# A four-stage hybrid kernel: the opening of its attention stage put in another order

## The chip, the cores and the metric

The kernel runs on one core of a Trainium2 chip. The metric is the device time of one execution in microseconds (us); lower is better. The core has five engines that each work through their own instruction list in order: TensorE (PE, matrix products and transposes), VectorE (DVE), ScalarE (ACT), GpSimd (POOL), and SyncE (SP), which here only issues DMA transfers. They wait for one another by semaphores.

## The reference

The input x has 4 x 1024 tokens of 256 channels. Four stages follow, each with a layer norm ahead and added to x: attention, a gated recurrence, a delta-rule stage, the recurrence again. Only attention is touched:

```python
c_kv = x @ W_dkv.T
q = (x @ W_dq.T @ W_uq.T).reshape(B, T, 16, 16)
q_lat = einsum('bqhd,hdl->bhql', q, k_eff)      # k_eff = (W_dq.T @ W_uq.T @ W_uk) per head
attn = softmax(causal(einsum('bhql,bkl->bhqk', q_lat, c_kv) / 4))
y_lat = einsum('bhqk,bkl->bhql', attn, c_kv)
y = einsum('bhql,hld->bqhd', y_lat, v_eff)
```

## The kernel before

The tokens are 8 groups of 512 (`GROUPS`), two to a batch row b. The 16 heads are taken four at a time (`HPU`); a unit u = (b, four heads), 16 units in all. Channels 0 to 127 (mt = 0) hold the heads of units 0 and 1 of a batch row, channels 128 to 255 (mt = 1) those of units 2 and 3.

**A group's projection** (`project(g)`) is a list of items: two "turn" (transposes of the normed tokens into a_xT), two "lat" (a_lat: two 512-column products of two steps each, n = 0 and 1), four "qk" (queries, which = 0, and keys, which = 1, for either mt; queries need lat 0, keys need lat 1), and two "v". Ahead of it a "norm" item: DVE takes statistics (`bn_stats`, `bn_aggr`, four of each), POOL turns them into four normed tiles.

**A qk item** is number i in the order in which the items come. PE writes it to a PSUM bank; ACT copies its leading bf16 part (`hi`, a_parts slot 0); DVE subtracts that (`rest`, into a_rest[i % 2]); ACT copies the middle part (`mid`, slot 1); POOL makes the last (`lo`, slot 2); SP sends the three parts from a_parts[i % 4] to memory (`parts_out`, 384 KB). `hi(i)` waits for `parts_out(i - 4)`, and `rest(i)` for `lo(i - 2)`.

**A unit's stack** (q_stack, k_stack: six bf16 partial products laid out over 96 rows) is loaded back from memory by `load(u, halves)` on SP: 12 transfers of 64 KB for one half of the tokens, of 128 KB for both. It waits until the parts of its groups have landed. A "max" item multiplies the stacks for a block of scores and DVE reduces the maxima: 38 items a unit, the first 11 of which need only half 0. "negmax" then turns the negated maxima (PE), splits them in three parts (DVE) and SP writes them into q_stack (`max_in`). After it come the scores, the exponentials (ACT) and the values.

**The order** is written out in `order()`: all engines walk the list `prologue` first, then the lists in `during`, one for each score step. The prologue holds the projections of groups 0 and 1, then 46 max items (all of unit 0, eight of unit 1) with the projections of groups 2 and 3 laid between, and the first negmax. Each engine takes from an item what is its own and keeps the list's order, so an engine that waits for one item holds up all behind it, DMA issues on SP included. Banks are dealt to items in turn, seven in the prologue.

DVE begins with two casts (`constants_vector`, L176 and L177), then three memsets of ones rows in k_stack (L777) and one of a PSUM bank (L778), and only then takes the first item.

Of the kernel before, what the change touches and what calls it, by code (L numbers as in the profile page):

```python
# [11 lines left out]
ACT = mybir.ActivationFunctionType  # L12
AXIS_X = mybir.AxisListType.X

P = 128
# [3 lines left out]
KT = C // P  # L19
# [5 lines left out]
NH, HS = 16, 16  # L25
HPU = 4
# [3 lines left out]
STACKS = 3  # L30
# [223 lines left out]
class Attention:  # L254
# [4 lines left out]
    WEIGHTS = (("wdqT", [P, KT, P]), ("wdkvT", [P, KT, P]), ("wuqT", [P, C]), ("wuq", [P, KT, P]),  # L259
               ("wuk", [P, KT, P]), ("wdq", [P, C]), ("wuv", [P, KT, P]), ("woT", [P, KT, C]))  # L260
    ARRIVES = {n: ("in_tokens", "in_keys", "in_values")[i // 3] for i, (n, _) in enumerate(WEIGHTS)}
    PROJECTED = tuple((which, mt) for which in range(2) for mt in range(KT))
    SPLIT = ((0, 1, 0, 1, 2, 0), (0, 0, 1, 1, 0, 2))
    PRODUCTS, ROWS, MAX_ROWS = 6, 6 * HS, 3
    LEAD = 8
# [52 lines left out]
    def order(self):  # L318

        per = len(self.pairs)  # L320
        maxima = []
        for u in range(len(self.units)):
            maxima += [("max", u, w) for w in range(per)]
        late = {}
        for u in range(len(self.units)):
            late[min((u + 1) * per + 2, len(maxima)) - 1] = ("negmax", u)

        def project(g):
            return ([("turn", g, kt) for kt in range(KT)] + [("lat", g, n) for n in range(2)] +
                    [("qk", g, *p) for p in self.PROJECTED] + [("v", g, j) for j in range(0, TPG, 2)])  # L330

        def take(n):
            out = []
            for i in range(self.taken, min(n, len(maxima))):
                out += [maxima[i]] + ([late[i]] if i in late else [])
            self.taken = max(self.taken, min(n, len(maxima)))
            return out

        self.taken, lead = 0, per + self.LEAD
        more = project(2) + [("norm", 4)] + project(3)  # L340
        self.prologue = [("norm", 0), ("norm", 1), ("const", 0), ("const", 1), ("const", 2)] + project(0) + [("norm", 2)]
        self.prologue += project(1) + [("norm", 3)]
        for i in range(lead):
            self.prologue += take(i + 1) + more[i * len(more) // lead:(i + 1) * len(more) // lead]
        self.score_bank, self.score_free, at = {}, {}, 0
        for n, heads in enumerate(self.scored):
            for i in range(len(heads)):
                self.score_bank[n, i] = self.SCORE_BANKS[at % 3]
                at += 1
        self.during = [[] for _ in range(len(self.steps) + 4)]  # L350
        for g in range(4, GROUPS):
            first = 4 + (g - 4) * 22
            for i, item in enumerate(project(g)):
                self.during[first + 2 * i].append(item)
            if g > 4:
                for j in range(2):
                    self.during[first - 8 + 2 * j].append(("norm", g, slice(2 * j, 2 * j + 2)))
        for n, (u, kb, qc) in enumerate(self.steps):
            self.during[n] += take(lead + -(-per * (n + 1) // len(self.unit_steps)))
            if kb == (qc + 1) * TPG - 1:  # L360
                self.during[n + 3].append(("out", u, qc))
        s, self.bank, self.released, held, at = self.s, {}, {}, {}, 0
        for ring, items in [(self.PROLOGUE_BANKS, self.prologue)] + [(self.RING, items) for items in self.during]:
            for item in items:
                if item[0] != "norm":
                    b = ring[at % len(ring)]
                    at += 1
                    self.bank[item] = b
                    self.released[item] = held.get(b)
                    held[b] = self.release(item)  # L370
            if items is self.prologue:
                for n, heads in enumerate(self.scored):
                    for i in range(len(heads)):
                        self.score_free[n, i] = held.get(self.score_bank[n, i])
                        held[self.score_bank[n, i]] = s["exp"](n, i)
# [13 lines left out]
        return s[{"turn": "xT_out", "lat": "lat_out", "v": "v_out", "max": "max_red", "negmax": "max_rest", "out": "att_o"}[kind]](*a)  # L389

    def part(self, g, which, mt):
        return (g * 2 + which) * KT + mt

    def stack_free(self, u):

# [21 lines left out]
    def sync(self, e, unmet):  # L417
        k, s, io = self.k, self.s, self.k.io

        def load(u, halves):  # L420
            b, g = self.units[u]
            st = u % STACKS
            cols = slice(halves[0] * BANK, (halves[-1] + 1) * BANK)
            sent = [s[f"parts_out{i % 4}"](i) for h in halves for i in range(self.part(2 * b + h, 0, 0), self.part(2 * b + h + 1, 0, 0))]
            for n in range(len(self.SPLIT[0])):
                for which, dst in ((0, self.qst[st]), (1, self.kst[st])):
                    src = io["parts"][which, self.SPLIT[which][n], g * HPU * HS:(g + 1) * HPU * HS,
                                      b * T + cols.start:b * T + cols.stop].rearrange("(h d) t -> d h t", h=HPU)
                    for w in unmet(self.stack_free(u), s["k_ones"](st), *sent):
                        e.wait_ge(*w)  # L430
                    e.dma_start(dst[n * HS:(n + 1) * HS, :, cols], src).then_inc(*s[f"stack_in{st}"].did(u, halves[-1], n, which))
# [25 lines left out]
        k.load_x_sync(e, range(2, GROUPS))  # L457
        for item in self.prologue:
            send(item)
            if item == ("qk", 0, *self.PROJECTED[-1]):  # L460
                load(0, (0,))
            if item == ("qk", 1, *self.PROJECTED[-1]):
                load(0, (1,))
                for u in range(1, STACKS):
                    load(u, (0, 1))
        for n, items in enumerate(self.during):
# [172 lines left out]
    def scalar(self, e, unmet):  # L639
        k, s, bank, w_ = self.k, self.s, self.k.bank, self.w  # L640

        def copy_out(item):
            kind, a = item[0], item[1:]
            if kind not in ("const", "turn", "lat", "qk", "v"):
# [14 lines left out]
            if kind == "turn":  # L659
                g, kt = a  # L660
# [3 lines left out]
            if kind == "lat":  # L664
                g, n = a
# [4 lines left out]
            if kind == "qk":  # L670
                i = self.part(*a)
                for w in unmet(s["qk_mm"](i), s[f"parts_out{i % 4}"](i - 4) if i >= 4 else None):
                    e.wait_ge(*w)
                if a[0] >= self.EARLY:
                    for w in unmet(s["lo"](i - 2)):
                        e.wait_ge(*w)
                    e.activation(self.rest[i % 2][:, :], out[:, :], ACT.Copy).then_inc(*s["raw"].did(i))
                    return
                e.activation(self.parts[i % 4][:, 0, :], out[:, :], ACT.Copy).then_inc(*s["hi"].did(i))
                for w in unmet(s["rest"](i)):  # L680
                    e.wait_ge(*w)
                e.activation(self.parts[i % 4][:, 1, :], self.rest[i % 2][:, :], ACT.Copy).then_inc(*s["mid"].did(i))
            if kind == "v":
                g, j = a
                for w in unmet(s["v_mm"](g, j), s["v_ones"]()):
                    e.wait_ge(*w)
                e.activation(self.v_rows[:, g * TPG + j:g * TPG + j + 2, :, 0:HS],
                             out[:, :].rearrange("p (i h d) -> p i h d", i=2, h=NH), ACT.Copy).then_inc(*s["v_out"].did(g, j))

        def exps(n, i):  # L690
            width, heads = self.span(n)[1], self.scored[n][i]
            for w in unmet(s["scores"](n, i), s["values"](n - 2) if n >= 2 else s["veff_mm"]()):
                e.wait_ge(*w)
            e.activation(self.weights[n % 2][:, heads[0]:heads[-1] + 1, 0:width],  # L694
                         bank[self.score_bank[n, i]][:, 0:len(heads) * width].rearrange("p (h x) -> p h x", h=len(heads)),
                         ACT.Exp, scale=HS ** -0.5).then_inc(*s["exp"].did(n, i))
# [21 lines left out]
    def vector(self, e, unmet):  # L718
        k, s, bank = self.k, self.s, self.k.bank
# [53 lines left out]
                                rs[:, :, :].rearrange("p i (h o) -> p i h o", o=1).to_broadcast([P, TPG, HPU, HS]), ALU.mult  # L773
                                ).then_inc(*s["att_o"].did(u, qc))

        for st in range(STACKS):
            e.memset(self.kst[st][self.ROWS:self.ROWS + self.MAX_ROWS, :, :], 1.0).then_inc(*s["k_ones"].did(st))  # L777
        e.memset(bank[7][:, :], 0.0).then_inc(*s["o_zero"].did())  # L778
        for item in self.prologue:
            take(item)  # L780
        for items in self.during:
            for item in items:
                take(item)
# [829 lines left out]
def build(nc, io):  # L1613
    with ExitStack() as ctx:
        k = Kernel(nc, ctx, io)
        attention = Attention(k)
        first = Ffn(k, "f1_", attention.updated, attention.ends())
        delta = Delta(k, first.updated, first.ends())
        second = Ffn(k, "f2_", delta.updated, delta.ends())
# [19 lines left out]
                stage.scalar(e, unmet)  # L1639

        def vector(e, unmet):
            k.constants_vector(e, unmet)
            for stage in stages:
                stage.vector(e, unmet)

# [69 lines left out]
```

## Time and profile before

| | |
|---|---|
| time before, median of 3 runs | 1452.52 us (1448.99 to 1452.66) |
| time of the profiled execution | 1452.64 us |
| its span in the trace | 1450.8 us |
| PE busy | 1218.1 us, 84% of the span |
| DVE busy | 880.1 us, 61% |
| ACT busy | 610.2 us, 42% |
| POOL busy | 447.5 us, 31% |

The span is the stretch that the profiler's rows cover; 1.84 us of the execution lie around it. The busy times are averages over stages that are limited by different things, so the opening, some 112 us, has to be read for itself.

### The profile page before, as it was taken

To read this page: it belongs to the slowest core of one execution; us is meant where nothing else is said; L and a number is where in the kernel's file an instruction comes from. 1 tells how busy PE (TensorE), PEld (TensorE's weight loads), DVE (VectorE), ACT (ScalarE), POOL (GpSimd) and SP (SyncE) were. 2 spreads that over 40 slices of the span, in tenths; PEclk is the share of its full clock that TensorE was granted. 3 is DMA by queue.
4 is the path that set the end of the run, shared out by engine and by line. 5 is a ranking of instruction groups with operands and counts; after the bars stand their busy time and mean duration, and the time that the engine had idled before them with its cause. 6 is when DMAs were issued, how large, how long until landed. Compare 5 with 4: busy or idle time off the path is not lost. (4 is left out here: it accounts for less than half of the span.)

```text
span 1450.8 us, 32359 instructions
## 1 busy us (share of the span) xinstructions
PE 1218.1 (84%) x13530; PEld 755.3 (52%) x13530; DVE 880.1 (61%) x1900; ACT 610.2 (42%) x1207; POOL 447.5 (31%) x663
## 2 busy tenths in 40 slices
PE   3779999999999999989999346566987858699993
PEld 1434444444444444337888323245665647488882
DVE  4466767676788777715434755677867362354346
ACT  1426666666666766655222322122332212142222
POOL 2420505142200000014231556443663313342304
PEclk7889999999999999999999768778999979899996
DMA  5492535344455333000000000011111100000003
GB/s 153 131 148 90 89 45 89 56 78 67 73 63 62 49 45 45 2 1 1 1 0 1 17 17 10 21 32 29 33 29 32 35 25 12 2 1 0 1 1 116
DMA packets 78754, 61.66 MB, mean 43 GB/s; under 512 B 41360, under 2 KB 65552, under 8 KB 78480
## 3 DMA queue, kind: packets, MB, share of 16 engines
q1 hardware_dynamic: 77456, 57.18, 21.9%
q10 hardware_dynamic: 1152, 2.41, 0.5%
q8 instruction: 106, 1.74, 0.5%
q14 instruction: 40, 0.33, 0.1%
HBM read 38.20 MB, written 20.97 MB: 41 GB/s over the span
## 5 line engine op out<-in xcount | busy, mean ns | idle before, releaser
L694 ACT ACTIVATE weights<-psum 128x512 f32<-128x512 f32 (+1 forms) x608 | 322.4, 585 | 159.4 <-PE psum L607 157.5
L739 DVE TENSOR_REDUCE maxima<-psum 128x1 f32<-128x512 f32 (+3 forms) x432 | 262.2, 662 | 57.4 <-PE psum L538 56.3
L607 PE MATMUL psum<-q_stack,k_stack 99*128 99x512 bf16 (+3 forms) x768 | 223.7, 328 | 1.3 <-ACT weights L694 1.1
L538 PE MATMUL psum<-k_stack,q_stack 96*128 96x512 bf16 (+3 forms) x768 | 213.0, 328 | 5.8 <-DMA k_stack<-qk_parts 4.1
L624 PE MATMUL psum<-weights,v_rows 128*17 128x512 f32 (+3 forms) x1536 | 162.0, 494 | 0.1
L510 POOL TENSOR_TENSOR residual<-residual,att_o 128x256 f32<-128x256 f32 x32 | 23.2, 725 | 364.0 <-DVE att_o L772 364.0
L900 PE MATMUL psum<-f_xT,f_weights_hi 128*128 128x512 f32 x384 | 123.5, 403 | 0.0
L739 DVE TENSOR_REDUCE negmax<-psum 128x1 f32<-128x384 f32 (+3 forms) x176 | 102.3, 634 | 27.8 <-PE psum L538 26.2
L607 PEld LDWEIGHTS psum<-q_stack,k_stack 99*128 99x128 bf16 x768 | 72.5, 98 | 83.1 <-ACT weights L694 38.6
L965 ACT ACTIVATE f_gates<-psum,ffn_biases 128x512 f32<-128x512 f32 x72 | 49.7, 690 | 155.8 <-PE psum L906 155.8
L1335 PE MATMUL psum<-d_w_qkb,d_hT 128*128 128x260 f32 x128 | 48.0, 510 | 68.3 <-DVE d_attnT_k_kb_v L1505 57.8
L538 PEld LDWEIGHTS psum<-k_stack,q_stack 96*128 96x128 bf16 x768 | 72.4, 99 | 56.9 <-issue 7.9
L906 PE MATMUL psum<-f_state_parts,f_weights_hi 128*128 128x512 f32 x288 | 90.4, 395 | 0.0
L603 PE MATMUL psum<-identity,mask_scores 128*128 128x128 bf16 (+2 forms) x352 | 87.1, 248 | 3.7 <-DMA q_stack<-max_parts 2.7
L534 PE MATMUL psum<-mask_scores,identity 128*128 128x128 bf16 (+2 forms) x352 | 86.7, 246 | 2.3 <-DVE a_rest L730 1.2
L603 PEld LDWEIGHTS psum<-identity,mask_scores 128*128 128x128 bf16 x352 | 34.0, 97 | 96.1 <-ACT weights L694 58.3
L900 PEld LDWEIGHTS psum<-f_xT,f_weights_hi 128*128 128x128 f32 x384 | 71.8, 191 | 16.2
L900 PE MATMUL psum<-f_xT,f_weights_lo 128*128 128x512 f32 x192 | 76.4, 398 | 0.0
L1340 PE MATMUL psum<-d_w_vg,d_hT 128*128 128x512 f32 x128 | 75.7, 724 | 0.0
L1335 PEld LDWEIGHTS psum<-d_w_qkb,d_hT 128*128 128x128 f32 x128 | 27.6, 239 | 77.0 <-DVE d_attnT_k_kb_v L1505 42.7
L1056 DVE COPY f_hidden<-psum 128x512 f32<-128x512 f32 x16 | 11.0, 690 | 91.4 <-PE psum L918 91.4
L906 PEld LDWEIGHTS psum<-f_state_parts,f_weights_hi 128*128 128x128 f32 x288 | 54.1, 188 | 13.3
(165 smaller groups left out, 2277.9 us busy)
## 6 DMA issues: line engine op xcount, KB each, us to landing
qk_parts<-a_parts SPq DMA_DIRECT2D x32, 384.0 KB, 3.6
q_stack<-qk_parts SPq DMA_DIRECT2D x90, 128.0 KB, 7.1
k_stack<-qk_parts SPq DMA_DIRECT2D x90, 128.0 KB, 7.8
residual<-in_x SPq DMA_DIRECT2D x8, 512.0 KB, 7.5
out_x<-residual SPq DMA_DIRECT2D x8, 512.0 KB, 3.8
ffn_weights<-in_ffn_w ACTq DMA_DIRECT2D x1, 2048.0 KB, 9.1
systems<-d_a_rows SPq DMA_DIRECT2D x32, 64.0 KB, 1.8
d_systems<-systems SPq DMA_DIRECT2D x4, 512.0 KB, 4.8
```

The lines of the kernel that those rows point to most:

```text
L534: e.matmul(out[:, 0:len(heads) * width].rearrange("p (h x) -> p h x", h=len(heads))[:, :, width - P:width], k.ident16[:, :], k.mask16[:, : ...
L538: m = e.matmul(out[:, i * width:(i + 1) * width], self.qst[st][0:self.ROWS, h, qb * P:(qb + 1) * P], self.kst[st][0:self.ROWS, h, k0:k0 + ...
L603: e.matmul(out[:, 0:len(heads) * width].rearrange("p (h x) -> p h x", h=len(heads))[:, :, 0:P], k.mask16[:, :], k.ident16[:, :].rearrange( ...
L607: m = e.matmul(out[:, j * width:(j + 1) * width], self.kst[st][0:self.ROWS + self.MAX_ROWS, h, kb * P:(kb + 1) * P], self.qst[st][0:self.R ...
L624: m = e.matmul(bank[7][32 * h:32 * h + HS + 1, off:off + width], self.v_rows[:, b * QB + kb, g * HPU + h, :], self.weights[n % 2][:, h, 0: ...
L694: e.activation(self.weights[n % 2][:, heads[0]:heads[-1] + 1, 0:width], bank[self.score_bank[n, i]][:, 0:len(heads) * width].rearrange("p ...
L739: e.tensor_reduce(to, bank[self.bank[item]][:, 0:len(heads) * width].rearrange("p (h x) -> p h x", h=len(heads)), AXIS_X, ALU.max, negate= ...
L900: m = e.matmul(bank[bk][:, :], w_hi_lo[wp][:, gate, kt, ms], x[:, v, kt, :], start=q == 0, stop=t == 0 and q == len(self.TERMS) - 1)
L906: m = e.matmul(bank[bk][:, :], w_hi_lo[wp][:, 4 + gate, kt, ms], self.state_parts[j][:, v, kt, :], start=False, stop=q == len(self.TERMS) - 1)
L965: e.activation(gs[:, gate, mt, :], next_bank()[:, :], func, bias=(k.ffn_b if t else self.bias0)[:, gate, mt:mt + 1]).then_inc(*s["gate"].d ...
L1335: m = e.matmul(qk_bank[:, 0:NQ + DH], cols[kt], self.w_qkb[:, kt, :], start=kt == 0, stop=kt == KT - 1)
L1340: m = e.matmul(vg_bank[:, :], cols[kt], self.w_vg[:, kt, :], start=kt == 0, stop=kt == KT - 1)
```

## The change

1. DVE takes the statistics of groups 0 and 1 first; casts and memsets come after them.
2. The projections of groups 0 and 1 are laid into one another, and the statistics of group 2 come earlier among them.
3. The four qk items of a group come in the order (queries mt 0, keys mt 0, queries mt 1, keys mt 1) instead of (queries 0, queries 1, keys 0, keys 1), and `part` numbers them so.
4. ACT's middle part of an item is put off until ACT has done the next item's leading part (or the next lat or v copy).
5. A stack's load waits only for the parts with its own channel half, two to a group instead of four, and unit 0's two loads are issued right behind the second qk item of groups 0 and 1.

```diff
-    PROJECTED = tuple((which, mt) for which in range(2) for mt in range(KT))
+    PROJECTED = tuple((which, mt) for mt in range(KT) for which in range(2))
...
-        self.prologue = [("norm", 0), ("norm", 1), ("const", 0), ("const", 1), ("const", 2)] + project(0) + [("norm", 2)]
-        self.prologue += project(1) + [("norm", 3)]
+        first, second = project(0), project(1)
+        self.prologue = [("norm", 0), ("norm", 1), ("const", 0), ("const", 1), ("const", 2)] + first[:4] + second[:2]
+        self.prologue += first[4:6] + second[2:4] + [("norm", 2)] + first[6:] + second[4:] + [("norm", 3)]
...
     def part(self, g, which, mt):
-        return (g * 2 + which) * KT + mt
+        return (g * KT + mt) * 2 + which
...
-            sent = [s[f"parts_out{i % 4}"](i) for h in halves for i in range(self.part(2 * b + h, 0, 0), self.part(2 * b + h + 1, 0, 0))]
+            mt = g * HPU * HS // P
+            sent = [s[f"parts_out{i % 4}"](i) for h in halves for i in (self.part(2 * b + h, which, mt) for which in range(2))]
...
-            if item == ("qk", 0, *self.PROJECTED[-1]):
+            if item == ("qk", 0, 1, 0):
                 load(0, (0,))
+            if item == ("qk", 1, 1, 0):
+                load(0, (1,))
             if item == ("qk", 1, *self.PROJECTED[-1]):
-                load(0, (1,))
                 for u in range(1, STACKS):
                     load(u, (0, 1))
...
+        behind = []
+
+        def middle():
+
+            for item in behind:
+                i = self.part(*item[1:])
+                for w in unmet(s["rest"](i)):
+                    e.wait_ge(*w)
+                e.activation(self.parts[i % 4][:, 1, :], self.rest[i % 2][:, :], ACT.Copy).then_inc(*s["mid"].did(i))
+            behind.clear()
...
                 e.activation(self.parts[i % 4][:, 0, :], out[:, :], ACT.Copy).then_inc(*s["hi"].did(i))
-                for w in unmet(s["rest"](i)):
-                    e.wait_ge(*w)
-                e.activation(self.parts[i % 4][:, 1, :], self.rest[i % 2][:, :], ACT.Copy).then_inc(*s["mid"].did(i))
+                middle()
+                behind.append(item)
+                return
...
+            middle()
...
-        for st in range(STACKS):
-            e.memset(self.kst[st][self.ROWS:self.ROWS + self.MAX_ROWS, :, :], 1.0).then_inc(*s["k_ones"].did(st))
-        e.memset(bank[7][:, :], 0.0).then_inc(*s["o_zero"].did())
         for item in self.prologue:
             take(item)
+            if item == ("norm", 1):
+                k.constants_vector(e, unmet)
+                for st in range(STACKS):
+                    e.memset(self.kst[st][self.ROWS:self.ROWS + self.MAX_ROWS, :, :], 1.0).then_inc(*s["k_ones"].did(st))
+                e.memset(bank[7][:, :], 0.0).then_inc(*s["o_zero"].did())
...
         def vector(e, unmet):
-            k.constants_vector(e, unmet)
             for stage in stages:
                 stage.vector(e, unmet)
```

VectorE, the start of its list (a minus is a row of before, a plus one of the change):

```order
+L221 BN_STATS ln_stats<-residual 128x6 x4
+L225 BN_AGGR ln_moments<-ln_stats 128x2 x4
+L221 BN_STATS ln_stats<-residual 128x6 x4
+L225 BN_AGGR ln_moments<-ln_stats 128x2 x4
 L176 CAST identity<-identity 128x128
 L177 CAST mask_scores<-mask_scores 128x128
-L777 MEMSET k_stack 3x4096 x3
-L778 MEMSET psum 128x512
-L221 BN_STATS ln_stats<-residual 128x6 x4
-L225 BN_AGGR ln_moments<-ln_stats 128x2 x4
-L221 BN_STATS ln_stats<-residual 128x6 x4
-L225 BN_AGGR ln_moments<-ln_stats 128x2 x4
```

Both groups' statistics moved from behind the memsets to the very start.

ScalarE, the parts of group 0 in the kernel before (a_parts with a number is the buffer; from psum is a leading part, from a_rest a middle part):

```order
L679 ACTIVATE a_parts0<-psum0 128x512 [waits a_qk_mm]
L682 ACTIVATE a_parts0<-a_rest0 128x512 [waits a_rest]
L679 ACTIVATE a_parts1<-psum0 128x512 [waits a_qk_mm]
L682 ACTIVATE a_parts1<-a_rest1 128x512 [waits a_rest]
L679 ACTIVATE a_parts2<-psum1 128x512 [waits a_qk_mm]
```

And after the change, the first items of group 1 (qk items 4, 5 and 6):

```order
L693 ACTIVATE a_parts0<-psum1 128x512 [waits a_parts_out0,a_qk_mm]
L693 ACTIVATE a_parts1<-psum2 128x512 [waits a_parts_out1,a_qk_mm]
L653 ACTIVATE a_parts0<-a_rest0 128x512 [waits a_rest]
L693 ACTIVATE a_parts2<-psum2 128x512 [waits a_parts_out2,a_qk_mm]
L653 ACTIVATE a_parts1<-a_rest1 128x512 [waits a_rest]
```

The middle part of an item now stands behind the leading part of the next: that of item 5 behind a wait for the transfer of item 2.

SyncE, from the first transfer of parts on, after the change (L441 sends parts, L433 loads a stack; before, all four parts went ahead of the loads):

```order
L441 DMA qk_parts<-a_parts0 128x3x512 [waits a_lo,a_mid,a_hi]
L441 DMA qk_parts<-a_parts1 128x3x512 [waits a_lo,a_mid,a_hi]
L433 DMA q_stack0<-qk_parts 16x4x512 [waits a_parts_out1,a_parts_out0,a_k_ones]
...
L441 DMA qk_parts<-a_parts2 128x3x512 [waits a_lo,a_mid,a_hi]
L441 DMA qk_parts<-a_parts3 128x3x512 [waits a_lo,a_mid,a_hi]
```

The parts of items 2 and 3 moved behind the 12 issues of unit 0's first load. The same follows in group 1: items 4 and 5, 12 issues, items 6 and 7, then 24 issues for units 1 and 2.

## Rows read from the trace of the kernel before

**Rows 1.** Windows: each engine's busy time, granted TensorE clock (PEclk), DMA share, rate.

```profile
58.20:98.90 40.70, 32.64 (x130) 16.18 (x128) 28.18 (x58) 13.39 (x24) 15.26 (x21) 0.87 0.91 138
98.90:104.70 5.80, 0.39 (x5) 0.13 (x3) 2.74 (x5) 1.71 (x3) 1.15 (x1) 0.86 0.79 259
140.00:500.00 360.00, 359.95 (x2694) 162.13 (x2692) 267.94 (x519) 238.85 (x453) 82.48 (x106) 1.00 0.45 66
```

**Rows 2.** Timeline of DVE, start and duration in us, the idle time before in brackets.

```profile
8.77 0.23 DVE L176 CAST identity<-identity 128x128 bf16<-128x128 f32 x1 [8.77 <-DMA identity_blocks<-in_constants]
...
22.17 0.48 DVE L778 MEMSET psum<- 128x512 f32 x1
22.68 1.40 DVE L221 BATCH_NORM_STATS2 ln_stats<-residual 128x6 f32<-128x256 f32 x4
...
25.57 0.36 DVE L225 BATCH_NORM_AGGREGATE ln_moments<-ln_stats 128x2 f32<-128x6 f32 x4
```

**Rows 3.** Timeline of PE, the same columns.

```profile
28.36 1.97 PE L248 MATMUL psum<-identity,normed 128*128 128x128 f32 x8 [13.82 <-POOL normed L240]
31.01 3.78 PE L579 MATMUL psum<-a_xT,a_wdqT 128*128 128x512 f32 x4 [0.69 <-ACT a_xT L663]
34.59 2.02 PE L579 MATMUL psum<-a_xT,a_wdkvT 128*128 128x512 f32 x4
...
74.80 0.82 PE L538 MATMUL psum<-k_stack,q_stack 96*128 96x512 bf16 x3 [4.07 <-DMA k_stack<-qk_parts]
...
104.70 0.37 PE L546 MATMUL psum<-identity,negmax 128*32 128x128 f32 x1 [5.42 <-DVE negmax L744]
...
112.36 0.38 PE L607 MATMUL psum<-q_stack,k_stack 99*128 99x512 bf16 x1
```

**Rows 4.** Timeline of SP, the issues of transfers (SPq).

```profile
49.23 0.33 SPq L431 DMA_DIRECT2D q_stack<-qk_parts  x1
...
65.71 0.32 SPq L431 DMA_DIRECT2D q_stack<-qk_parts  x1
...
71.23 0.42 SPq L431 DMA_DIRECT2D q_stack<-qk_parts  x1
...
82.81 24.77 SPq L439 DMA_DIRECT2D qk_parts<-a_parts  x6
107.69 1.87 SPq L447 DMA_DIRECT2D q_stack<-max_parts  x3
```

**Rows 5.** Transfer issued at 82.81: size, us to landing.

```profile
qk_parts<-a_parts SPq DMA_DIRECT2D x1, 384.0 KB, 18.4
```

**Rows 6.** Timeline of ACT around the wait of qk item 12.

```profile
101.29 0.60 ACT L679 ACTIVATE a_parts<-psum 128x512 bf16<-128x512 f32 x1 [5.20 <-DMA qk_parts<-a_parts]
...
106.81 0.60 ACT L679 ACTIVATE a_parts<-psum 128x512 bf16<-128x512 f32 x1 [0.95 <-PE psum L586]
```

**Rows 7.** Transfers of tokens to residual issued before 1.7 us, with landing times.

```profile
L192 SPq DMA_DIRECT2D residual<-in_x x2: 427/462/497, 0.7 to 1.2; - x2
DMA to landing us min/median/max: 4.7/5.4/6.0
```

**Rows 8.** Timeline of POOL, the two first norms.

```profile
24.46 0.24 POOL L232 TENSOR_SCALAR ln_rstd<-ln_moments 128x4 f32<-128x4 f32 x1 [22.68 <-DVE ln_moments L225]
...
30.06 2.17 POOL L240 TENSOR_SCALAR normed<-residual,ln_negmean,ln_rstd 128x256 f32<-128x256 f32 x4
```

**Rows 9.** Timeline of all engines, qk item 0 through its parts.

```profile
37.50 0.60 ACT L679 ACTIVATE a_parts<-psum 128x512 bf16<-128x512 f32 x1 [0.26 <-PE psum L586]
...
38.13 0.69 DVE L730 TENSOR_TENSOR a_rest<-psum,a_parts 128x512 f32<-128x512 f32 x1 [12.20 <-ACT a_parts L679]
...
38.85 0.63 ACT L682 ACTIVATE a_parts<-a_rest 128x512 bf16<-128x512 f32 x1 [0.76 <-DVE a_rest L730]
...
39.63 1.16 POOL L496 TENSOR_TENSOR a_parts<-a_rest,a_parts 128x512 bf16<-128x512 f32 x1 [7.41 <-ACT a_parts L682]
```

**Rows 10.** Transfer of parts issued between 41.5 and 43.5: size, us to landing.

```profile
qk_parts<-a_parts SPq DMA_DIRECT2D x1, 384.0 KB, 2.6
```

## The prediction

> **What bounds the kernel now.** I read the windows first. From 140 to 500 us PE is busy for 359.95 of 360 us at full clock [rows 1]: what comes earlier at the end of the opening stays earlier. In the opening PE idles, and the timeline of PE gives four waits that matter [rows 3]: 13.82 us until 28.36, for POOL's normed tiles; 4.07 until 74.80, for the second half of unit 0's stack; 5.42 until 104.70, for DVE; and none right before the first scores at 112.36. I follow each back.
>
> The first: DVE starts its first statistics at 22.68, because the block from the cast at 8.77 to the end of the PSUM memset at 22.65 stands ahead of them [rows 2], though the two groups' tokens had landed at 0.7 + 4.7 = 5.4 and 1.2 + 6.0 = 7.2 [rows 7].
>
> The second: SP issues the load only at 65.71, when group 1's parts had landed; 9.1 us later the stack is there.
>
> The third names DVE, but DVE stood at `rest(12)`, which waited for ACT's `hi(12)`, and ACT had waited 5.20 us, until 101.29, for the transfer of parts 8 [rows 6], which frees the buffer. SP issued that at 82.81, behind the 24 issues for units 1 and 2 that began at 71.23 [rows 4], and it took 18.4 us to land [rows 5], at 101.2, while the DMA engines were 91% busy at 138 GB/s [rows 1]. So the opening's end hangs on one chain: tokens, statistics, POOL, projections of groups 0 and 1, their parts, half 1's load, 24 stack transfers, parts 8, `hi(12)`. I work that chain out in the new order.
>
> **Statistics first.** Two groups' statistics take 22.68 to 25.93, 1.65 each [rows 2]. They now run 5.4 to 7.1 and 7.2 to 8.9. The block of 13.9 us follows, 8.9 to 22.8. POOL starts 0.1 after each and took 24.46 to 32.23 for two norms [rows 8], 3.9 each: now done at 11.1 and 15.0. PE is free at 28.36 - 13.82 = 14.54, so it turns group 0 at 14.5: 13.8 earlier, and POOL has 3.4 to spare.
>
> The moved block now lies beside POOL's work, and no row of before has a k_stack memset beside POOL. Bounds: nothing, or both wait for each other fully; then norm 1 would be ready at 22.8 + 3.9 = 26.7. I take nothing, since group 1's tiles aren't wanted before 20.7 (below), 5.7 after 15.0. The Trainium skill (SBUF — State Buffer, "Who interferes with whom") speaks against the casts: a copy or cast in a two-port mode and a GpSimd instruction shut each other out. No row here shows it; the casts last about 0.45 together, and by that rule POOL would be some 0.5 late, inside its 3.4, so the sum would not change. The same section says that a DVE instruction with at most one SBUF input outside those modes doesn't contend, which would leave the memsets harmless.
>
> **Projections laid together.** From turn to lat PE took 2.65 (28.36 to 31.01); then lat 0 took 3.58 at half clock and the next one some 1.75 at full [rows 3]. Now PE comes straight out of the weight products instead of a gap, so I take full clock from 17.2 (bound: 1.8 later). Lat products to 20.7, group 1's turns 0.9, qk items 0 and 1 0.86 each: 23.3; group 1's lats to 26.7. `hi(0)` falls at 22.6, `rest(0)` at 23.2, just behind the memsets (22.8): here the block has no cover left, and another microsecond in it costs a microsecond.
>
> **Middle parts behind.** Before, an item went hi 0.60, rest 0.69, mid 0.63 in turn, then lo 1.16 on POOL [rows 9]. Now `hi(1)` runs at 23.4 beside `rest(0)`, `mid(0)` at 24.0; the lat copy at 25.1 is ahead of `mid(1)`, 25.7; `lo(1)` ends at 27.6. Its parts land 2.6 after the issue [rows 10], at 30.4. Unit 0's first load takes 12 issues, 71.23 - 65.71 = 5.5 [rows 4]: to 35.9. Landing of the half: about 39, PE having idled from 35.
>
> The new waits: parts 2, whose `lo` (behind norm 2 on POOL, 27.6 to 31.5) ends at 32.7, are issued only at 36.0, behind the 12. I give them 4.4 to land behind that traffic, 40.4 (bounds 2.6 [rows 10] and 18.4 [rows 5]; nearer the first, since only 12 transfers of 64 KB lie ahead, not 24 of 128). `hi(6)` waits for that, and behind it on ACT stands `mid(5)`: 41.1 to 41.7, `lo(5)` to 43.0, landed at 45.7. Item 5 is the last that half 1 needs, no longer item 7, so the load starts at 45.8 in place of 65.71: 19.9 earlier. Half 1 is there 9.1 later, 54.9 for 74.80. PE gets there at about 53.6, so the stall stays, at 1 to 2 us.
>
> **The DMA chain.** Before, from 74.80 to 101.2 the engines moved the rest: 26.4. The same 24 transfers come again, but now with parts 6 and 7 ahead, which can't go before half 1's 12 issues: 0.77 MB, 3.0 at the 259 GB/s of the window that moved parts [rows 1]; I take 2.3, as that window holds idle time too (bounds 0 and 5.2, two landings of 2.6). Parts 8 land at 54.9 + 2.3 + 26.4 = 83.6. Their own `lo`, though put off, is long done. `hi(12)` starts at 83.7 for 101.29: 17.6 earlier. PE comes to its wait 19.9 earlier, so this wait grows from 5.4 to 7.7, and takes back 2.3.
>
> **The tail.** `mid(13)` now stands behind `hi(14)`, which came at 106.81 on the old clock of time [rows 6]: mid to 108.0, lo to 109.3, its send, and only then the three max_parts issues, about 109.8 for 107.69 [rows 4]. PE came to the scores at 112.36 with no idle. Cost between 0 and 2.1; I take 0.8.
>
> **Sum**: -17.6 + 0.8 = -16.8. From the profiled execution's 1452.64: 1435.8. That execution is 0.1 from the median, 1452.52, so the forecast is 1436. The last part of the change also lets the loads of units 3 to 15 wait for two parts a group instead of four; that gains nothing, as PE doesn't wait there [rows 1].
>
> **Rivals.**
> - *Only the head start counts.* The new waits (parts 2 behind 12 issues, `mid(5)` behind `hi(6)`) eat what the interleaving gives. For it: each is a real wait in the new order; against: the load leaves out items 6 and 7. -13.8 + 0.8: 1439.6. Chance 0.13.
> - *POOL and the memsets shut each other out.* Norm 1 at 26.7, wanted at 20.7: +6.0, 1441.8. It begins to cost when norm 1 is over 5.7 late. Chance 0.08.
> - *DMA isn't the limit.* If the 24 transfers drain sooner, PE's own 19.9 holds: 1432.7. Against it: 91% busy. Chance 0.12.
> - *Slower: the clock.* PE now has more short gaps (35 to 39, 40 to 44). If it stayed at half clock through the opening: the 32.64 busy us at 0.87 between 58.20 and 98.90 [rows 1] become 57, +24, less the wait of 7.7: +16.5; groups 0 and 1 hold some 16 us at full clock, doubled, less 8 of waits: +8. Total -16.8 + 24.5 = +7.7: 1460.3. It turns to slower once it costs over 16.8 net. Against it: before, with a gap of 13.82 just behind it, PE was at full clock after about 6 us of work [rows 3]. Chance 0.03.
> - *No change:* the later stages wait for something that doesn't move. Against it: 359.95 of 360. 1452.6, chance 0.04.
>
> **The numbers.** The forecast has 0.60, and its own range, from the 1.8 of the clock, the bounds of parts 6 and 7 and the tail, is 1433.5 to 1438.5. With the first three rivals the range is 1431.5 to 1442. About 0.3% (4.4 us) is what a measurement tells from no change: faster 0.60 + 0.13 + 0.08 + 0.12 = 0.93, same 0.04, slower 0.03.
>
> **What would show it.** In the changed profile: first statistics at 5.4; PE's first turn at 14.5; the first stack load issued near 30.4, half 1's near 45.8; PE released for half 1 near 55; ACT released by parts 8 near 83.7; first scores near 95.5; from there all rows shifted alike. If `hi(6)` waits much past 40, or norm 1 ends past 20.7, or parts 8 land late after half 1, that step was wrong.

## The result, and the profile after

The changed kernel takes 1428.59 us (median of 4 runs, 1427.9 to 1432.31) against 1452.16 us of the kernel before, timed beside it. The ratio is 0.9845, 95% interval 0.9822 to 0.9867: 19 to 26 us faster. The direction was as forecast, the size was not: -16.8 was forecast, and the median lies under the range's lower end of 1431.5. The profiled execution took 1432.31, 20.3 less than that of before. Medians and ratios are of executions in the chip's faster state; one execution of a later variant (e6), 1605.08 us at a granted clock of 0.74, was in its slower one and is left out.

The page's first lines of the changed kernel, busy time by engine:

```profile
span 1430.4 us, 32356 instructions
PE 1218.3 (85%) x13530; PEld 756.3 (53%) x13530; DVE 881.0 (62%) x1900; ACT 610.5 (43%) x1207; POOL 447.1 (31%) x663
```

PE worked 1218.1 us before: the work is the same, and what went is idle time. Windows of the changed kernel (PE, PEld, DVE, ACT, POOL busy, granted TensorE clock, DMA share, rate), of the opening's head and of the saturated stretch, to be read beside [rows 1]:

```profile
14.50:28.30 13.80, 13.06 (x44) 6.93 (x43) 10.60 (x15) 8.10 (x16) 3.93 (x6) 1.00 0.49 159
116.00:476.00 360.00, 359.95 (x2687) 161.98 (x2686) 267.06 (x516) 239.65 (x455) 81.76 (x105) 1.00 0.44 65
```

The 13.8 us in which PE had idled now hold 13.06 busy us at full clock. DVE's timeline, which answers to [rows 2]:

```profile
5.04 1.41 DVE L221 BATCH_NORM_STATS2 ln_stats<-residual 128x6 f32<-128x256 f32 x4 [5.04 <-DMA residual<-in_x]
...
21.80 0.48 DVE L797 MEMSET psum<- 128x512 f32 x1
22.31 1.47 DVE L745 TENSOR_TENSOR a_rest<-psum,a_parts 128x512 f32<-128x512 f32 x2
```

`rest(0)` follows the last memset without a gap, at 22.31 where 23.2 was forecast. PE's timeline, which answers to [rows 3]:

```profile
13.91 1.48 PE L248 MATMUL psum<-identity,normed 128*128 128x128 f32 x8
16.13 1.98 PE L582 MATMUL psum<-a_xT,a_wdqT 128*128 128x512 f32 x4 [0.74 <-ACT a_xT L677]
...
44.96 3.78 PE L582 MATMUL psum<-a_xT,a_wdqT 128*128 128x512 f32 x4
...
52.42 0.81 PE L541 MATMUL psum<-k_stack,q_stack 96*128 96x512 bf16 x3
...
83.74 0.37 PE L549 MATMUL psum<-identity,negmax 128*32 128x128 f32 x1 [7.71 <-DVE negmax L759]
...
92.19 0.23 PE L606 MATMUL psum<-identity,mask_scores 128*128 128x128 bf16 x1 [1.91 <-DMA q_stack<-max_parts]
```

The wait of 4.07 for half 1 is gone, the wait at the negmax has grown from 5.42 to 7.71, and a new one of 1.91 stands ahead of the first scores. Group 2's first lat products, at 44.96, ran at half clock: PE was busy for 1.86 of the 5 us from 33 to 38, and the granted clock was 0.59 from 38 to 42 and 0.50 from 42 to 46. In the kernel before the same rows took less:

```profile
64.62 2.43 PE L579 MATMUL psum<-a_xT,a_wdqT 128*128 128x512 f32 x4
```

This cost nothing on the chain: half 1's stack landed at 51.7 (3.2 us after its last issue, at 48.53), and PE, still at work, took it up at 52.42. Last issue of half 1's load in the changed kernel, size and us to landing, then that of before, issued at 70.76:

```profile
k_stack<-qk_parts SPq DMA_DIRECT2D x1, 64.0 KB, 3.2
k_stack<-qk_parts SPq DMA_DIRECT2D x1, 64.0 KB, 4.0
```

SP and ACT, which answer to [rows 4] and [rows 6], first SP:

```profile
34.92 6.26 SPq L441 DMA_DIRECT2D qk_parts<-a_parts  x4
...
43.48 0.32 SPq L433 DMA_DIRECT2D q_stack<-qk_parts  x1
```

and ACT:

```profile
38.34 0.60 ACT L693 ACTIVATE a_parts<-psum 128x512 bf16<-128x512 f32 x1 [5.24 <-DMA qk_parts<-a_parts]
...
80.33 0.60 ACT L693 ACTIVATE a_parts<-psum 128x512 bf16<-128x512 f32 x1 [7.49 <-DMA qk_parts<-a_parts]
```

Both waits of ACT for transfers are the forecast ones: `hi(6)` for parts 2, with `mid(5)` behind it, and `hi(12)` for parts 8.

### The profile page after: what moved, and what is told of

Its sections match the earlier page's. It is cut to its first block and busy times, and to the rows that moved or that the text cites. A ratio compares the mean times of both kernels' runs of the same rounds, so it can differ in the third digit from the quotient of the medians.

```text
span 1430.4 us, 32356 instructions
## 1 busy us (share of the span) xinstructions
PE 1218.3 (85%) x13530; PEld 756.3 (53%) x13530; DVE 881.0 (62%) x1900; ACT 610.5 (43%) x1207; POOL 447.1 (31%) x663
## 5 line engine op out<-in xcount | busy, mean ns | idle before, releaser
L513 POOL TENSOR_TENSOR residual<-residual,att_o 128x256 f32<-128x256 f32 x32 | 23.2, 725 | 364.1 <-DVE att_o L787 364.1
L1352 PEld LDWEIGHTS psum<-d_w_qkb,d_hT 128*128 128x128 f32 x128 | 27.6, 239 | 76.2 <-DVE d_attnT_k_kb_v L1522 38.8
```

Source lines behind the costliest of these rows:

```text
L1352: m = e.matmul(qk_bank[:, 0:NQ + DH], cols[kt], self.w_qkb[:, kt, :], start=kt == 0, stop=kt == KT - 1)
```

## The experiments

Marks of all kernels, from the timelines: the issue of half 1's load, the start of `hi(12)`, PE's wait at the negmax transpose (L549, before L546), the start of the first exponential; the rest of the profiled span behind that; and the ratio to the kernel before, from runs timed side by side.

| kernel | half 1 issued | hi(12) | PE waits | first exp | behind it | ratio (95%) |
|---|---|---|---|---|---|---|
| before | 65.71 | 101.29 | 5.42 | 113.91 | 1336.9 | 1 |
| changed | 43.48 | 80.33 | 7.71 | 92.68 | 1337.7 | 0.9845 (0.9822-0.9867) |
| changed, again (e5) | 43.56 | 80.48 | 7.71 | 92.59 | 1331.3 | 0.9813 (0.9791-0.9835) |
| statistics only (e1) | 49.15 | 83.78 | 5.94 | 96.50 | 1337.1 | 0.9894 (0.9869-0.9919) |
| all but statistics (e11) | 59.96 | 96.84 | 9.11 | 109.81 | 1340.1 | 0.9955 (0.9937-0.9973) |
| no deferral (e2) | 43.16 | 80.03 | 9.01 | 92.45 | 1336.4 | 0.9845 (0.9827-0.9862) |
| no interleaving (e3) | 43.37 | 80.10 | 8.74 | 92.24 | 1338.7 | 0.985 (0.9832-0.9868) |
| loads late, four parts (e4) | 49.14 | 84.87 | 3.87 | 96.96 | 1339.1 | 0.9885 (0.9866-0.9904) |
| loads late, two parts (e10) | 44.21 | 80.19 | 6.32 | 92.34 | 1336.0 | 0.9834 (0.9806-0.9863) |
| one memset more (e8) | 47.38 | 84.27 | 10.12 | 96.39 | 1339.3 | 0.9865 (0.9843-0.9887) |
| unit 2 later (e6) | 43.84 | 74.43 | 0.68 | 85.23 | 1335.5 | 0.9795 (0.9766-0.9824) |
| unit 2 later, no deferral (e7) | 43.10 | 72.98 | 1.26 | 84.67 | 1335.6 | 0.9786 (0.9753-0.9818) |
| unit 2 last, no deferral (e9) | 43.42 | 73.43 | 1.26 | 83.93 | 1333.5 | 0.98 (0.9777-0.9823) |

The column behind the first exponential runs from 1331.3 to 1340.1, and the two profiles of the one changed kernel lie 6.4 apart in it. So what an edit does to the opening is read from the marks, and differences of a few us between total times say little.

### Statistics first, alone (e1_stats_only)

The kernel before, with this alone (the memsets follow `constants_vector`, as in the change):

```diff
         for item in self.prologue:
             take(item)
+            if item == ("norm", 1):
+                k.constants_vector(e, unmet)
...
```

> The kernel before with one part of the change alone: DVE's statistics of groups 0 and 1 ahead of the casts and memsets. My theory (one chain through the opening, each part of the change shortens a piece of it): the first turn at 13.9 us, full clock in the first lat products, rest(0) held by the memsets at 22.3 in place of 38.13, so half 1's load is issued near 50 (65.71 before), the first scores come 15 to 16 us earlier, and the time is 1436 to 1438. Rival (the head start is all, interleaving and halves give nothing): this kernel reaches the time of the changed one, 1428 to 1432.

Measured: ratio 0.9894, 1436.59 us median, as the chain theory said; the rival is out. In its trace lat 0 starts at 15.81 and PE's clock is full (in [rows 3] 31.01 and half clock); group 1's, behind 5.70 us without work, runs near half clock again (granted 0.52):

```profile
15.81 1.98 PE L579 MATMUL psum<-a_xT,a_wdqT 128*128 128x512 f32 x4 [0.74 <-ACT a_xT L663]
31.24 3.68 PE L579 MATMUL psum<-a_xT,a_wdqT 128*128 128x512 f32 x4 [5.70 <-ACT a_xT L663]
```

The first exponential comes 17.4 earlier, more than the 14.5 of PE's first turn (13.83 for 28.36).

### All but the statistics (e11_all_but_stats)

The changed kernel with this undone, the memsets again at the head of DVE's list:

```diff
+        k.constants_vector(e, unmet)
...
         for item in self.prologue:
             take(item)
-            if item == ("norm", 1):
-                k.constants_vector(e, unmet)
...
```

> The changed kernel with the casts and memsets ahead of the statistics again, all else as changed. The statistics alone brought the first exponential from 113.91 to 96.50, and the rest from there to 92.6. If the two pieces add up, it comes near 110 here and the time is 1448 to 1451; if the rest only pays behind the head start (or the head start only with the rest), it stays within 1 us of 113.9, or falls under 108.

Measured: first exponential 109.81, 4.1 earlier than before. 17.4 + 4.1 = 21.5, and the whole change has 21.2: the two add up. The median, 1446.44, is a little under what was expected.

### Without the deferral of the middle part (e2_no_deferral)

```diff
-                middle()
                 behind.append(item)
-                return
```

> The changed kernel with ACT's middle part right behind its leading part again. Theory: mid(5) no longer stands behind hi(6), which waited 5.24 us for parts 2; lo(5) ends near 36 in place of 41.9, half 1's load is issued near 41 in place of 43.48, and the wait of 1.91 for max_parts before the first scores goes: 2 to 5 us faster than the changed kernel, 1424 to 1427. Rival (putting the middle part off shortens the projections, as ACT doesn't wait for DVE between the two): 1 to 3 us slower than the changed kernel.

Measured: ratio 0.9845, the same as the changed kernel's, median 1430.92. Neither theory held for the time. Half 1's load was issued at 43.16, only 0.3 earlier. SP's timeline shows why:

```profile
35.28 2.87 SPq L441 DMA_DIRECT2D qk_parts<-a_parts  x4
43.16 0.32 SPq L433 DMA_DIRECT2D q_stack<-qk_parts  x1
```

Parts 2 to 5 are now all issued by 38.2, but they land 3.4, 3.9, 4.6 and 6.1 us after their issues, the last near 43: four transfers of 384 KB come one upon the other behind the 12 of the first load. In the changed kernel the deferral made parts 5 late (issued last, near 40.8, they landed 2.6 later), without it the queue does, and the two are within 0.3 us. The wait of 1.91 for max_parts did go: PE shows none before the first scores.

### Without the interleaving of groups 0 and 1 (e3_no_interleave)

```diff
-        self.prologue = [("norm", 0), ("norm", 1), ("const", 0), ("const", 1), ("const", 2)] + first[:4] + second[:2]
-        self.prologue += first[4:6] + second[2:4] + [("norm", 2)] + first[6:] + second[4:] + [("norm", 3)]
+        self.prologue = [("norm", 0), ("norm", 1), ("const", 0), ("const", 1), ("const", 2)] + first + [("norm", 2)]
+        self.prologue += second + [("norm", 3)]
```

> The changed kernel with the projections of groups 0 and 1 one after the other, and group 2's norm between them, as before. Theory: parts 2 and 3 are ready before the 12 issues end either way and half 1's load stays within 2 us of 43.48: the time stays within 2 us of the changed kernel, 1427 to 1431. Rival (the interleaving carries what goes beyond the head start): half 1's load near 49, 4 to 6 us slower, 1433 to 1435.

Measured: ratio 0.985, half 1's load at 43.37, first exponential 92.24. The theory held: the interleaving is worth nothing by itself, as SP has 12 issues to make either way (28.85 to 34.4) before it sends parts 2.

### The loads' place and what they wait for (e4_loads_late, e10_late_but_two)

e4 puts back both, the parts waited for (the `sent` line) and the place (the others); e10 has only the others:

```diff
-            sent = [... for i in (self.part(2 * b + h, which, mt) for which in range(2))]
+            sent = [... for i in range(self.part(2 * b + h, 0, 0), self.part(2 * b + h + 1, 0, 0))]
...
-            if item == ("qk", 0, 1, 0):
+            if item == ("qk", 0, *self.PROJECTED[-1]):
                 load(0, (0,))
-            if item == ("qk", 1, 1, 0):
-                load(0, (1,))
             if item == ("qk", 1, *self.PROJECTED[-1]):
+                load(0, (1,))
```

> The changed kernel with loads that wait for all four parts of a group and stand behind its last qk item, as before. Theory: unit 0's first load is issued near 36 in place of 29.3, half 1's near 46.5 in place of 43.48, those of units 1 and 2 start near 52 in place of 50: 2 to 3 us slower than the changed kernel, 1430 to 1432. Rival (the loads' place doesn't matter, as the later DMA wait hides it): no difference, 1428 to 1429.

> The changed kernel with unit 0's loads in their old place behind the last qk item of a group, but still waiting only for the two parts of their channel half. It splits what the kernel with late loads that wait for four had in one. If the number of parts waited for matters: half 1's load near 43 to 44, first exponential within 1 us of 92.6, about 1428. If the place matters: half 1's load near 49 and first exponential near 97, as with both, about 1436.

Measured: e4's first exponential is 4.3 later than the changed kernel's, ratio 0.9885, more than expected; e10's is 0.3 earlier, ratio 0.9834, as the first of its theories said. SP's rows of e4:

```profile
41.10 2.81 SPq L441 DMA_DIRECT2D qk_parts<-a_parts  x4
49.14 0.32 SPq L433 DMA_DIRECT2D q_stack<-qk_parts  x1
```

and of e10:

```profile
39.46 2.86 SPq L441 DMA_DIRECT2D qk_parts<-a_parts  x4
44.21 0.32 SPq L433 DMA_DIRECT2D q_stack<-qk_parts  x1
```

With all four of a group to wait for, half 1's load starts 5.2 after the last of four issues ends; with two it starts 1.9 after. So the gain is carried by the statistics ahead and by a load that waits only for its own channel half. The order of the qk items, part 3 of the change, is what brings the two parts of a half together; no run undoes it by itself. Without the short wait parts 2 to 4 bring nothing: e4 has the first exponential at 96.96, the kernel with the statistics alone at 96.50.

### One memset more (e8_memset_twice)

```diff
+                e.memset(self.kst[0][self.ROWS:self.ROWS + self.MAX_ROWS, :, :], 1.0).then_inc(*s["k_pre"].did())
+                for w in unmet(s["k_pre"]()):
+                    e.wait_ge(*w)
                 for st in range(STACKS):
```

> The changed kernel with one more k_stack memset (4.3 us) in DVE's block behind the statistics. Theory: rest(0) stood right behind the block (22.31 after an end at 22.28), so all of it is passed on: rest(0) near 26.6, half 1's load near 47.7, the time 4 us longer, 1432 to 1433. Rival (a later wait, the transfers of parts 2 or the traffic of the stacks, swallows it): under 1.5 us longer.

Measured: `rest(0)` starts at 26.74 instead of 22.31 (4.4 later), half 1's load at 47.38 (3.9), `hi(12)` 84.27 (3.9), the first exponential 96.39 (3.7). DVE's timeline:

```profile
22.65 3.47 DVE L799 MEMSET k_stack<- 3x4096 bf16 x1 [0.80 <-issue]
26.22 0.48 DVE L800 MEMSET psum<- 128x512 f32 x1
26.74 1.29 DVE L745 TENSOR_TENSOR a_rest<-psum,a_parts 128x512 f32<-128x512 f32 x2
```

The chain passes a delay at its head on to its end nearly whole. The time itself, 1435.9 (1432 to 1433 expected), is 9.2 above the changed kernel's median timed beside it (e5). The opening holds 3.7 of that; behind the first exponential, where the edit does nothing, this profile is 1.6 and 8.0 us longer than the two of the changed kernel.

### Unit 2's load later (e6_unit2_later, e7_unit2_later_no_deferral, e9_unit2_last)

If `hi(12)` waits for the transfers queued ahead of parts 8, moving 12 of the 24 behind must free it. e6 and e7 move unit 2's load as shown, e9 behind the whole prologue:

```diff
             if item == ("qk", 1, *self.PROJECTED[-1]):
-                for u in range(1, STACKS):
-                    load(u, (0, 1))
+                load(1, (0, 1))
+            if item == ("qk", 2, *self.PROJECTED[-1]):
+                load(2, (0, 1))
```

e7 and e9 leave out the deferral too.

> The changed kernel with unit 2's load issued behind group 2's parts instead of ahead of them. Theory (the opening ends with the transfers queued ahead of parts 8): parts 8 land near 66, hi(12) doesn't wait, the 7.71 us wait of PE before the negmax transposes goes, and the first scores come 7 to 9 us earlier: 1420 to 1422. Rival (the DMA engines' total work is the limit, so the wait only moves to max_parts, which now queue behind unit 2's 12 transfers): 0 to 3 us faster, 1426 to 1429.

> As the kernel with unit 2's load behind group 2's parts, and also with the middle part right behind the leading one. Theory: max_parts no longer stand behind a late mid(13): another 1 to 2 us, 1418 to 1421. Rival (the deferral is worth nothing here either way): the same as that kernel.

> The middle part right behind the leading one, and unit 2's load moved behind the whole opening (after max_parts and parts 12 to 15). In the kernel with that load behind group 2's parts the first scores still waited 2.11 us for max_parts, which were queued behind unit 2's 12 transfers. Theory (transfers queued ahead are what each of these waits is): that wait goes too, the first exponential comes near 82.5 in place of 84.67, unit 2's stack is still there before its first max item, and the time is 1417 to 1421. Rival (PE's own work of the opening is now the limit): no earlier than 84.5, the time as before that move.

Measured: ratios 0.9795 (0.9766 to 0.9824), 0.9786 (0.9753 to 0.9818), 0.98 (0.9777 to 0.9823); medians 1425.6, 1422.5 and 1424.3, each above the time that its theory named; first exponentials 85.23, 84.67, 83.93, in place of 92.6. e9's 83.93 lies between its theory's 82.5 and its rival's 84.5. ACT has no wait for parts 8 left, and the negmax wait of 7.71 is 0.68, 1.26 and 1.26. PE of e6:

```profile
77.26 0.27 PE L550 MATMUL psum<-identity,negmax 128*32 128x128 f32 x1 [0.68 <-DVE negmax L760]
...
84.56 0.23 PE L607 MATMUL psum<-identity,mask_scores 128*128 128x128 bf16 x1 [0.74 <-DMA q_stack<-max_parts]
```

and of e9:

```profile
76.84 0.27 PE L549 MATMUL psum<-identity,negmax 128*32 128x128 f32 x1 [1.26 <-DVE negmax L757]
...
82.99 0.23 PE L606 MATMUL psum<-identity,mask_scores 128*128 128x128 bf16 x1 [0.47 <-DMA q_stack<-max_parts]
```

The DMA queue was the limit of the opening: with half its load out of the way PE's opening ends 7.5 to 8.7 earlier. How much of that reaches the total isn't settled. All three ratios lie under both of the changed kernel's (0.9845 and 0.9813), and they can't be told from one another; the intervals of e6 and e9 just touch its first (from 0.9822), e7's does not, and all three overlap its second. Timed side by side, e6's median is 1.1 us and e7's 4.2 us under the changed kernel's 1426.7.

### The changed kernel once more (e5_same_again)

> The changed kernel once more, nothing edited, to learn how much of its time belongs to the single execution. If the forecast's steps were only short in size, the first exponential is again near 92.7 us, and the times lie between 1427 and 1432; if the first profile was an odd one, the opening's marks (half 1's load at 43.5, parts 8 at 80.3) move by more than 1 us.

Measured: ratio 0.9813, median 1426.68, runs from 1425.53 to 1432.06. The marks of the opening agree within 0.2 us. The spans do not: 1430.4 and 1423.9. Windows of the delta-rule stage, first of the changed kernel's first profile:

```profile
827.90:1111.20 283.30, 208.08 (x4436) 138.48 (x4437) 197.26 (x562) 71.12 (x213) 146.10 (x274) 0.85 0.11 25
```

and of the second:

```profile
825.80:1105.80 280.00, 205.02 (x4435) 136.97 (x4436) 196.40 (x562) 71.14 (x213) 146.58 (x274) 0.86 0.12 25
```

The same 4,435 or so PE instructions take 283.30 and 280.00 us. Another 1.6 us arise right behind the opening, between the first exponential and the first copy of values (`att_oT`): 13.0 us in the first profile, 11.4 in the second, and 11.0 to 11.6 in all others. There the granted clock differs, first profile and then second:

```profile
94.00:96.00 2.00, 2.00 (x9) 0.89 (x7) 1.37 (x3) 1.20 (x3) 0.00 (x0) 0.50 1.01 391
94.00:96.00 2.00, 2.00 (x17) 1.05 (x19) 2.00 (x5) 2.00 (x5) 0.00 (x0) 1.00 1.03 400
```

From the first `att_oT` to the last both take 517.1. The rest, 0.4 and 1.1, lies ahead of the delta-rule stage and behind it. Both profiles are of one kernel, so none of this is the edit's.

## Why the prediction was wrong in its size

**The chain was right.** Its links show in the trace, in the forecast order, and e8 shows that from `rest(0)` on it is one chain. One forecast wait did not come: PE was to stall for 1 to 2 us at half 1, but the stack landed at 51.7 for 54.9 and PE, there at 52.42 for 53.6, did not wait at all. **The lengths were too long**, and nearly all erred the same way:

| step | forecast | measured | own error |
|---|---|---|---|
| first turn on PE | 14.5 | 13.91 | -0.6 |
| unit 0's first load issued | 30.4 | 29.33 | -0.5 |
| parts 2 landed, hi(6) | 40.4 | 38.34 | -1.0 |
| half 1's load issued | 45.8 | 43.48 | -0.3 |
| half 1 landed | 54.9 | 51.7 | -0.9 |
| parts 8 landed, hi(12) | 83.7 | 80.33 | -0.2 |
| first scores | 95.5 | 92.19 | +0.1 |

**The step that failed is the landings of transfers, in size.** The term most mis-sized is that of parts 2: "I give them 4.4 to land behind that traffic". The changed trace has, for the transfer issued at 34.92 (size, us to landing):

```profile
qk_parts<-a_parts SPq DMA_DIRECT2D x1, 384.0 KB, 3.3
```

Next is half 1's load, "9.1 later" in the forecast and 43.48 to 51.7, 8.2, measured. The first turn and the projections, 1.1 together, are the rest: `lo(1)` ended at 26.6 for 27.6. The drain of the 24 transfers, 26.4 + 2.3 = 28.7 in the forecast, took 28.6 from half 1's landing to `hi(12)`, as forecast. The sum up to `hi(12)` is -21.0 where -17.6 was forecast; at the first scores it is -20.1 for -16.8. That is nearly the whole error for the profiled execution: 1435.8 forecast, 1432.31 measured.

Full clock from the first lat product was right (1.98 us for four rows that took 3.78), the clock's bound of 1.8 wasn't needed. That the wait at the negmax would grow to 7.7, as measured, came out by luck, two equal errors: PE came to it 23.3 earlier, not 19.9, and the wait ended 21.0 earlier, not 17.6. The tail's +0.8 was right in sum, not in its parts: PE waited 1.91 for max_parts, but had come 1.1 sooner.

**The range failed too.** "1433.5 to 1438.5" took in the bounds of the clock, of parts 6 and 7 and of the tail, but not the bound of 2.6 that the prediction itself had set for parts 2; and neither it nor the lower end of 1431.5 had a term for how far one execution lies from the next, though 4.4 us is named there as what a measurement can tell. e5 shows 6.5 us between two profiles of the same kernel. The profiled execution, 1432.31, lies inside the wider range; the median, 1428.59, 3.7 lower, does not.

**The rivals.** "Only the head start counts" priced the head start at 13.8, and the whole at 1439.6. e1 has 1436.59: PE's first turn comes 14.5 earlier, the full clock of the first lat product adds 1.8, `rest(0)` comes at 22.17 for 38.13, half 1's load 16.6 and the first exponential 17.4 earlier. What it said of the rest is half right: interleaving (e3) and deferral (e2) bring nothing; but the loads' shorter wait brings 4 (e4, e10, e11). The forecast had credited that to item 5 instead of 7 being the last, which is the same thing. "POOL and the memsets shut each other out" is out: beside the memsets the second norm's four tiles took as long as in [rows 8]. POOL of the changed kernel:

```profile
8.49 2.23 POOL L240 TENSOR_SCALAR normed<-residual,ln_negmean,ln_rstd 128x256 f32<-128x256 f32 x4
...
12.47 2.17 POOL L240 TENSOR_SCALAR normed<-residual,ln_negmean,ln_rstd 128x256 f32<-128x256 f32 x4
```

2.17 as before, beside the memset that ran from 13.95. The first four took 2.23, and beside them lay the two casts, at 8.40 and 8.54, and the start of a memset; that is 0.06 more, not the duration of a cast. DVE's rows:

```profile
8.40 0.23 DVE L176 CAST identity<-identity 128x128 bf16<-128x128 f32 x1
8.54 0.22 DVE L177 CAST mask_scores<-mask_scores 128x128 bf16<-128x128 f32 x1
...
13.95 3.47 DVE L796 MEMSET k_stack<- 3x4096 bf16 x1 [0.80 <-issue]
```

This agrees with the Trainium skill (SBUF — State Buffer, "Who interferes with whom") as far as the memsets go; its lock by casts shows at most as those 0.06, and no row tells whether these casts ran in a two-port mode. "DMA isn't the limit" named a time, 1432.7 (without the tail's 0.8), that was nearer than mine, for a reason that e6 refutes: DMA was the limit, and taking 12 transfers out of it brought the first exponential 7.5 us forward. "The clock" came for stretches only: from about 38 to 49, where it cost the chain nothing, and at 94 to 96 in the first profile, with 1.6 us. "No change" did not come.

**What stays open**: the medians differ by 23.6, the first exponentials by 21.2. One piece of the rest shows in the profiles: from the first `att_oT` to the last the kernel before takes 519.3 us and both profiles of the changed one 517.1, with no difference in the first 369. But e8 takes 519.4 there, and the kernel with the statistics alone 520.0, so whether these 2 us belong to the change or are scatter is not shown.

## What to carry to other kernels

When an engine's list begins with work that nobody waits for yet, such as memsets of buffers used much later, put the first link of the longest chain ahead of it, and count what the earlier start does to the clock as well. A load should wait for the pieces that it reads, not for all that are written with them; that was worth 4 us in the opening here, and two reorderings of compute nothing. Where an engine waits for a small transfer's buffer, look at what was queued ahead of it: moving loads that are wanted late behind it brought the end of the opening 7 us further forward, without touching an instruction of the compute engines, though the total time has not clearly followed. And a range worked out from one trace needs a term for how far two executions of one kernel lie apart.

## What the runs showed of the hardware

- Four parts transfers of 384 KB issued within 3 us behind 12 stack loads had the last land 6.1 and 6.2 us after its issue (e2, e4), while one alone takes 2.6 [rows 10]. Without the deferral it is this queue that fixes the start of half 1's load.
- Two profiled executions of one kernel, their marks alike within 0.2 us for the first 93 us, ended 6.5 us apart. In 1.6 us of it one had a granted clock of 0.50 at 94 to 96 us and the other 1.00.
- Parts of 384 KB queued behind 24 stack loads of 128 KB took 17.8 us to land (issued at 62.44), and 11.7 with 12 of the loads moved away (e6, issued at 57.10).
- Where PE's turn came straight behind other work, at 13.91, its lat products ran at full clock from 16.13 (four rows in 1.98); after 13.8 us without work, the same took 3.78 [rows 3].
